# Row block 0 loaded and mapped in two halves of 256 rows, and column 0 of six row blocks begun on the first half

## What is computed

```python
x1  = layernorm(x + adj @ (x * (u >= 0.1) / 0.9))
m   = tanh(|x1|) * x1 / (|x1| + 1e-8)             # per row, |x1| clipped to 10
s   = adj @ m
out = arctanh(|s|) * s / (|s| + 1e-8)             # |s| clipped to 0.999
y   = layernorm(x1 + out @ weight + bias)
```

## Time and profile before

| | us |
|---|---|
| Median of 3 runs (lowest, highest) | 941.54 (941.12, 941.77) |
| The profiled execution, its own time | 944.53 |
| Its span in the profile | 941.9 |
| PE busy in the span | 898.6 (95%) |
| DVE busy | 287.2 (30%) |
| ACT, POOL busy | 52.2, 57.4 (6%, 6%) |
| Read from HBM | 355.57 MB, 380 GB/s over the span |

### The profile page before, as it was taken

The page is one execution under the profiler, slowest core; times in us unless marked ns, Lnnn a source line. Parts: engine busy times, 40 slices in busy tenths (PEclk is TensorE's granted clock), DMA queues, the critical chain, the costliest instruction groups (busy, mean ns, idle before and its releaser), DMA issues.

```text
span 941.9 us, 10555 instructions
## 1 busy us (share of the span) xinstructions
PE 898.6 (95%) x4224; PEld 301.8 (32%) x4224; DVE 287.2 (30%) x1056; ACT 52.2 (6%) x136; POOL 57.4 (6%) x50
## 2 busy tenths in 40 slices
PE   5579999999999999999999999999999999999994
PEld 1113333333333333333333333333333333333331
DVE  1136463422314130303131130403104030057565
ACT  0001010000000000000000000000000000002332
POOL 0000000000000000000000000000000000003232
PEclk9999999999999999999999999999999999999998
DMA  9999999999999999997979899898998999999993
GB/s 380 418 422 421 422 421 416 421 422 422 419 421 422 421 414 421 347 424 257 422 274 400 347 336 373 323 422 344 372 358 303 424 347 354 310 402 420 421 421 134
DMA packets 52319, 358.35 MB, mean 380 GB/s; under 512 B 6320, under 2 KB 8368, under 8 KB 9392
## 3 DMA queue, kind: packets, MB, share of 16 engines
q1 hardware_dynamic: 49536, 355.59, 93.5%
q10 hardware_dynamic: 2736, 2.10, 0.7%
HBM read 355.57 MB, written 2.10 MB: 380 GB/s over the span
## 4 chain that ended last, share of the span: by engine, by line
PE 85%; DMA 12%; SPq 2%; DVE 1%; issue 0%; POOL 0%; ACT 0%; DVEq 0%
PE sums_both L697 38%; PE sums_part L660 19%; PE sums_first L651 19%; DMA ring<-adj_dram 12%; PE sums_part L651 3%; PE sums_part L679 3%; PE sums_both L679 3%; SPq L339 1%; SPq L335 0%; PE sums_first L741 0%; PE sums_both L741 0%; PE sums_both L736 0%; POOL rooted L379 0%; POOL rooted L360 0%; DVE rows_in L603 0%
## 5 line engine op out<-in xcount | busy, mean ns | idle before, releaser
L697 PE MATMUL sums_both<-ring,feats 128*64 128x512 f32 x1696 | 370.2, 592 | 0.7 <-DMA ring<-adj_dram 0.7
L651 PE MATMUL sums_first<-ring,feats 128*64 128x512 f32 x1088 | 245.9, 598 | 27.7 <-DMA ring<-adj_dram 27.7
L697 PEld LDWEIGHTS sums_both<-ring,feats 128*64 128x64 f32 x1696 | 122.8, 137 | 242.3 <-issue 239.3
L660 PE MATMUL sums_part<-ring,feats 128*64 128x512 f32 x816 | 183.1, 593 | 1.0 <-issue 1.0
L651 PEld LDWEIGHTS sums_first<-ring,feats 128*64 128x64 f32 x1088 | 77.0, 138 | 190.0 <-issue 141.0
L487 DVE TENSOR_TENSOR row_saved<-sums_both,row_saved 64x512 f32<-64x512 f32 x15 | 10.2, 682 | 350.7 <-ACT row_saved L421 350.7
L660 PEld LDWEIGHTS sums_part<-ring,feats 128*64 128x64 f32 x816 | 59.3, 137 | 115.3 <-issue 114.7
L370 POOL TENSOR_TENSOR rooted<-base,power 128x8 f32<-128x8 f32 x16 | 27.8, 1736 | 801.1 <-DVE base L513 801.1
L552 DVE TENSOR_TENSOR rows_in<-sums_part,rows_in 128x512 f32<-128x512 f32 x36 | 24.9, 692 | 134.3 <-PE sums_part L660 134.2
L651 PE MATMUL sums_part<-ring,feats 128*64 128x512 f32 x240 | 55.9, 596 | 3.0 <-DMA ring<-adj_dram 3.0
L421 ACT COPY row_saved<-sums_first 64x512 f32<-64x512 f32 x16 | 9.3, 580 | 607.2 <-PE sums_first L651 607.2
(11 more groups left out here) (72 smaller groups left out, 246.6 us busy)
## 6 DMA issues: line engine op xcount, KB each, us to landing
ring<-adj_dram SPq DMA_DIRECT2D x331, 1024.0 KB, 12.9
rows_in<-xu_dram SPq DMA_DIRECT2D x8, 512.0 KB, 20.0
feats<-adj_dram SPq DMA_DIRECT2D x4, 1024.0 KB, 18.9
out_dram<-rows_in ACTq DMA_DIRECT2D x15, 128.0 KB, 7.5
out_dram<-rows_in SPq DMA_DIRECT2D x1, 96.0 KB, 1.9
selw<-selector_dram ACTq DMA_DIRECT2D x1, 32.0 KB, 6.7
selw<-weight_dram ACTq DMA_DIRECT2D x1, 32.0 KB, 10.3
bias_sb<-bias_dram ACTq DMA_DIRECT2D x1, 32.0 KB, 12.4
```

What stands on the lines that cost most here:

```text
L651: last = nc.tensor.matmul(bank[at:at + F], feats[:, which, c * TB + t, :], block_of(slot)[:, t, :], start=start and t < 2, stop=stop and t ...
L660: last = nc.tensor.matmul(bank[F * g:F * g + F], feats[:, 1, c * TB + t, :], block_of(slot)[:, t, :], start=start and t == 0, stop=stop an ...
L697: last = nc.tensor.matmul(sums_both[r % 2][layer * F:layer * F + F], feats[:, layer, c * TB + t, :], block_of(slot)[:, t, :], start=begin ...
```

## The change

Row block 0 is stored on the host in another layout: for each pair of columns and each half of 256 rows, a block of 1 MB. The first eight loads (`top`) hold rows 0 to 255 of all columns, the next eight rows 256 to 511, each with 8 matmuls of 256 columns; each half has a `turn` of its own with two tiles of 128 rows. After both, column 0 of rows 2 to 7 is begun on the first half of mapped rows (`begin`, 4 matmuls on the first half of the block, a load of 0.5 MB) in six different PSUM banks, and completed on the second (`complete`, the other 0.5 MB). The lead of row block 1 is dropped; `early` remains for rows 8 to 15. The held columns 0 to 3 of row 0 lie in pairs in two slots each, released after the odd column. Later re-reads of row 0 (`strip`) fetch two pieces of 4 KB for each partition. Early sums of the first product are no longer transposed and added to x: ACT copies them as they are into the part of `feats` that their rows will fill later, and DVE adds them at the join, before the row's last blocks are in.

```diff
+BEGUN = (2, 3, 4, 5, 6, 7)
+HALF = BS // 2
+HALF_TILES = TB // 2
@@ work_order
         if r == 0:
-            order += firsts + holds + [("turn", 0)]
+            for h in range(2):
+                order += [("top", 0, pair, h) for pair in range(NB // 2 - 1, -1, -1)] + [("turn", 0, h)]
+            order += [("begin", row, 0) for row in BEGUN] + [("complete", row, 0) for row in BEGUN]
             continue
-        lead, rest = lead_of([("both", r, c) for c in range(r >= 2, r - 1)] + firsts)
+        lead, rest = ([], firsts) if r == 1 else lead_of([("both", r, c) for c in range(r >= 2, r - 1)] + firsts)
...
-            early = [("early", row, 0) for row in range(2, NB)]
+            early = [("early", row, 0) for row in range(BEGUN[-1] + 1, NB)]
@@ place_blocks
+            if kind == "top":
+                h = step[3]
+                kept[r, c, h] = place("block", 0, 2 * c + h)
+                own = [kept[r, c, h]]
+                if c >= HELD[0] // 2:
+                    done += own
...
+            elif kind == "begin":
+                own = [place("lower", r, c)]
+                kept[r, c] = own[0]
+            elif kind == "complete":
+                own = [kept.pop((r, c))]
+                loads.append(("upper", r, c, own[0][0], 0))
+                done += own
@@ SP
-                sp.dma_start(block_of(slot), adj[r, c]).then_inc(block_loaded[slot], 16)
+                if kind == "block":
+                    sp.dma_start(block_of(slot), adj[r, c]).then_inc(block_loaded[slot], 16)
+                if kind == "strip":
+                    own = slice(c % 2 * HALF_TILES, (c % 2 + 1) * HALF_TILES)
+                    sp.dma_start(block_of(slot).rearrange("p (h t) w -> p h (t w)", h=2),
+                                 adj[0, c - c % 2:c - c % 2 + 2, :, own, :].rearrange("h p t w -> p h (t w)")
+                                 ).then_inc(block_loaded[slot], 16)
+                if kind == "lower":
+                    sp.dma_start(ring[:, slot, 0:HALF_TILES, :],
+                                 adj[r, c, :, 0:HALF_TILES, :]).then_inc(block_loaded[slot], 16)
+                if kind == "upper":
+                    sp.dma_start(ring[:, slot, HALF_TILES:TB, :],
+                                 adj[r, c, :, HALF_TILES:TB, :]).then_inc(rest_loaded[r], 16)
@@ ACT
-                if step[0] == "early":
+                if step[0] in ("complete", "early"):
 
                     act.wait_ge(block_released, uses[i][1])
-                    nc.scalar.copy(support[half(r), r // 2], early_banks[r % 2][F:P]).then_inc(early_saved, 1)
+                    nc.scalar.copy(early_sums(r)[0:F], early_bank(r)[0:F, 0:HALF])
+                    nc.scalar.copy(early_sums(r)[F:P], early_bank(r)[0:F, HALF:BS])
+                    nc.scalar.copy(support[half(r), r // 2], early_bank(r)[F:P]).then_inc(early_saved, 1)
@@ DVE
+            def early_join(i, r):
+
+                dve.wait_ge(early_saved, saved_at[r])
+                dve.wait_ge(block_released, uses[i][1])
+                for h in range(2):
+                    w = slice(h * HALF, (h + 1) * HALF)
+                    last = V.tensor_tensor(row_sum[:, w], sums_both[r % 2][0:F, w], early_sums(r)[F * h:F * h + F], ALU.add)
+                done(last)
...
-            def early_end(i, r):
-                dve.wait_ge(block_released, uses[i][1])
-                turn(early_banks[r % 2][0:F].rearrange("p (t n) -> p t n", n=P)).then_inc(early_turned, 1)
-                dve.wait_ge(early_turned, r - 1)
-                done(V.tensor_tensor(x_row(r), turned[:], x_row(r), ALU.add))
@@ PE
+                if kind == "top":
+                    h = step[3]
+                    pe.wait_ge(dropped, 1 + chunk_order.index(c))
+                    for col in (2 * c, 2 * c + 1):
+                        for t in range(TB):
+                            at = F * (t % 2)
+                            last = nc.tensor.matmul(sums_first[h][at:at + F, 0:HALF], feats[:, 0, col * TB + t, :],
+                                                    pack_of(slot)[:, col % 2, t, :],
+                                                    start=col == NB - 2 and t < 2, stop=col == 1 and t >= TB - 2)
...
+                if kind in ("begin", "complete", "early"):
...
+                    if kind == "complete":
+                        pe.wait_ge(rest_loaded[r], 16)
+                    pe.wait_ge(mapped, turn_of(0, kind != "begin"))
+                    for t in range(HALF_TILES if kind == "complete" else 0, HALF_TILES if kind == "begin" else TB):
```

More of the change, by code:

```diff
@@ L166, in place_blocks, with place @@
     times = [0] * (SLOTS + SPARES)
-    turned = spares = 0
+    placed = turned = spares = 0
+    def place(kind, r, c):
+        nonlocal placed
+        assert placed < SLOTS or placed - SLOTS < len(freed), "every slot is held"
+        slot = placed if placed < SLOTS else freed[placed - SLOTS]
+        times[slot] += 1
+        loads.append((kind, r, c, slot, max(0, placed - SLOTS + 1)))
+        placed += 1
+        return slot, times[slot]
     for i, step in enumerate(order):
@@ L173, in place_blocks @@
         rows, c = step[1:3]
-        held = []
+        held, done = [], []
         for r in rows if kind == "part" else (rows,):
-            if kind == "part" and step[6]:
-                slot, nth = kept.pop((r, c))
-            else:
[L179 to L190, removed]
+            if kind == "top":
[4 more added lines that the diff above has]
+                    done += own
+            elif kind == "part" and step[6] and r == 0:
+                own = [kept[0, c // 2, h] for h in range(2)]
+                if c % 2:
+                    done += own
+            elif kind == "part" and step[6]:
+                own = [kept.pop((r, c))]
+                done += own
+            elif kind == "begin":
+                own = [place("lower", r, c)]
+                kept[r, c] = own[0]
+            elif kind == "complete":
+                own = [kept.pop((r, c))]
+                loads.append(("upper", r, c, own[0][0], 0))
+                done += own
+            else:
+                own = [place("block" if r else "strip", r, c)]
+                if kind == "hold":
+                    kept[r, c] = own[0]
+                else:
+                    done += own
+            held.append(own)
+        freed += [slot for slot, _ in done]
+        count = len(done)
+        if turned == NB + 1 and kind == "part" and not spares:
             spares = SPARES
             freed += range(SLOTS, SLOTS + SPARES)
-        uses[i] = held, len(freed)
+            count += SPARES
+        uses[i] = held, len(freed), count
     return loads, uses
@@ L204, in build @@
     chunk_order = []
[L205 removed]
+    for _, _, c, _, _ in loads[:NB]:
         if c * TB // CHUNK not in chunk_order:
@@ L226, in saved_through, with turn_of @@
     def saved_through(r):
-        return min(1 + 2 * r, 2 + r)
+        return r + 3
+    def turn_of(r, h=1):
+        return r + h + 1
+    saved_at = {row: k + 1 for k, row in enumerate(s[1] for s in order if s[0] in ("complete", "early"))}
+    unsignalled = [i for i, (_, _, count) in uses.items() if order[i][0] == "part" and not count]
     with ExitStack() as es:
```

182 lines of the change are left out of this document (113 added, 69 removed).

## The result

| | before | after |
|---|---|---|
| Median of the runs (lowest, highest), us | 941.65 (941.12, 942.10), 4 runs | 946.49 (945.28, 948.49), 4 runs |
| Ratio after / before, 95% interval | | 1.0051 [1.0039, 1.0062] |
| The profiled execution, its own time | 944.53 | 945.28 |
| Its span | 941.9 | 943.4 |

The change makes the kernel slower by 0.51%, 4.8 us, outside the range that was given. So medians are compared with medians here, and profiles by the time of "both 4 1", the step at the gate.

The account below looks back on a forecast made before the run. A full DMA queue up to the landing of block (4, 1) at 206.63 us was taken to bound the kernel. Median 941.54 us, + 0 for the idle time, + 0.36 for smaller transfers, gave 941.9 us; range 940.0 to 944.5 us.

Parts of the forecast that it names:

- the gate: Landing of block (4, 1), load 77, at 206.63 us; PE can't be further at "both 4 1" than the bytes before it.
- What bounds it: Full DMA queue for the first 345 us, so block (4, 1) landing at 206.63 us sets PE's time; gain there 0.
- The idle time moves and is not removed: PE's 4 to 5 us saved after 53 us return as 5 to 5.5 us of waits before 207 us; net 0.
- Mapping, early sums, ACT, DVE, slots, 256-column matmuls at no cost: Row 0's mapping in halves, early sums, shared slots and shorter matmuls: each covered by lead or idle time, cost 0.
- Smaller transfers: Early halves before "both 4 1" and later re-reads of row 0: 0.18 us each, +0.36 us in sum.
- that block lands when it did: Block (4, 1), before "both 4 1": same bytes ahead in a never dry queue, so unchanged landing but for smaller transfers' cost.
- rival 3: Small pieces cost more, before "both 4 1" and in the tail: +3.0 us, 944.5 us; chance 0.09.
- The bound from above: Smaller transfers priced like output stores, 1.21 times as much per MB: 0.25 us a half, 6.0 us for 24.
- rival 4: The fixed cost of each of six added transfers stands open: 11.4 us more, 952.9 us; chance 0.02.
- Rival 1: PE's 4.95 us of idle time between 53.25 and 73.5 us is really removed: 936.6 us; chance 0.06.
- The unexplained pause: One block between 53.25 and 56.85 us took 1.11 us too long; it may fall away or come twice: 940.4 to 943.0 us.

Follow-up runs that it names:

- e6: Kernel before with blocks (1, 6) and (1, 7) left out of the loads but for 64 bytes a partition: 936.58 us, ratio 0.995.
- e11: Changed kernel with half blocks stored as closed runs and re-reads of row 0 in runs of 8 KB: 941.53 us, 1.0003 to before.
- e3: Changed kernel with the six early blocks loaded whole and re-reads of row 0 from a closed second copy: 941.68 us, 1.0004 to before.
- e4: Kernel before with column 0 of rows 2 to 7 fetched as two halves, one right behind the other: 941.66 us, ratio 1.0001.
- e10: Changed kernel with the early halves read in the same order from a copy with 12 KB between partition rows: 943.29 us, 1.0018 to before.
- e5: Changed kernel with each early half block stored as a closed run of 512 KB, order kept: 943.33 us, 1.0014 to before.
- e1: Changed kernel with each of the six early blocks loaded whole, in one transfer of 1 MB: 943.24 us, 1.0011 to before.
- e7: Changed kernel with each second half of an early block loaded right behind its first half: 942.72 us, 1.0014 to before.
- e2: Changed kernel with row 0 re-read from a second copy in runs of 8 KB, early halves unchanged: 944.48 us, 1.0033 to before.
- e12: e11 with column 1 of rows 11 to 15 moved from behind the gate to before it: 937.75 us, 0.9964 to before.

## Why the prediction was wrong

**What bounds it: right.** The queue to block (4, 1) sets the time (e6: -4.84 us at the gate, -4.8 us at the end), and whatever is lost behind it comes on top.

**The idle time moves and is not removed: right.** PE runs without a break from 56.02 to 76.6 us; in the profile of after it waits 7.4 us for DMA before 345 us instead. Some eight short waits between 140 and 207 us were expected: after has 11 with 5.6 us there, since the late gate adds its share, and e11, where the gate is in place, has 9 with 4.4 us.

**Mapping, early sums, ACT, DVE, slots, 256-column matmuls at no cost: right.** No wait of PE for ACT or DVE; the second half's last mapped rows were written at 63.78 us, where 64.8 was allowed. The timeline of PE in after, at the last `top` step and the first `begin`:

```profile
54.24 1.95 PE L788 MATMUL sums_first<-ring,feats 128*64 128x256 f32 x16 [0.54 <-DMA ring<-adj_dram]
56.02 3.60 PE L804 MATMUL sums_both<-ring,feats 128*64 128x512 f32 x16
```

Eight matmuls of 256 columns took 1.78 us to the next start, where four of 512 take 1.72: 0.06 us of the 1.1 us allowed. e3 shows that all these together are free, to within the 0.1% of its interval.

**Smaller transfers: the step that failed.** The term was +0.36 us, 0.015 for each of 24 halves, "because the nearest row has the very size of piece". The whole change measures +4.8 us, and e3 and e11, which differ from after in these transfers alone, are within 0.2 us of before: all of it stands in this term. The size was right and was not what counted: e4 has the same halves at no cost. I had taken "size of the transfer" for the property of which the price depends, and the x and u pieces for the nearest row, though they stand singly between whole blocks and have a pitch of 32 KB. The halves of the change read every other 4 KB, and come six first ones in a row and then six second ones. In 54 to 74 us that cost 8.41 - 7.75 = 0.66 MB against before, 1.6 us at 421 GB/s, and 17.63 - 15.32 = 2.3 us against e10 and e5. With it fell the sentence "that block lands when it did": it landed 3.8 us later in the profile, of which e1, e5, e7 and e10 take back 3.2 to 4.0. About 3.2 us of the median are the halves; the rest, 1.6 us, is put down to the re-reads, six of which were priced at 0.18 us. As a mechanism this is nearest to rival 3, whose +3.0 us stood at 0.09, but not as it was put: the cost is no fixed price of each piece, it falls on a few of the twelve halves and, smaller, on the re-reads behind the gate. The bound from above in the prediction, 6.0 us, held; the choice of 0.36 within it failed.

**The fixed cost of added transfers (rival 4, 952.9 us): wrong.** e4 adds six transfers to before and e7 adds six to e1: +0.2 us (ratio 1.0001), and -0.5 us. The figure of about 2 us behind this rival, from the Trainium skill, "DMA: Bandwidth & Descriptors", section "Anatomy of one DMA", is given there for DMAs issued from GpSimd; these are issued from SP. **Rival 1 (936.6 us): wrong,** as e11 shows, which removes the idle time and ends at 941.53.

**The unexplained pause** between 53.25 and 56.85 us coincides with a fetch of instructions. The DMA queues of before, 54 to 56 us:

```profile
q1 hardware_dynamic: 114, 0.81, 98.5%
q8 instruction: 1, 0.02, 3.4%
```

The fetch is one packet of 16 KB that took 3.4% of 16 x 2 us = 1.1 us, which is the 1.11 us by which the block was late. That a block waits for its slowest engine would explain it, but no run isolates it, and most fetches go without such a pause: before has five more of 16 KB until 187 us, and beside them one block is 0.3 us late and no other by more than 0.2; e5, e7 and e10 have one at 53.2 to 53.4 us and lose at most 0.2 us there.

**Where the 3.8 us at the gate lie,** by landing times: after's 16 blocks of row 0 were in 1.0 us later than before's (54.20 against 53.21 us), the next 7 MB took 1.6 us more, although they lack before's pause of 1.1 us, and the 54 blocks from there to the gate 1.2 us more. In that last part two landings of after are 3.15 and 3.31 us behind the one before, at 159.87 and 193.03 us; e2 has the same two (3.16 and 3.35), while e5, e7 and e10 have none over 2.7 us there. Fetches of instructions started at 157.9 and 189.1 us in after, but the other kernels have fetches near there too. So e5, e7 and e10 take back these 1.4 us as well, and why is not shown.

**Open.** The mechanism in the memory; why stalls among the halves are followed by two more pauses 90 and 120 us later; and how much of the re-reads' 1 to 2 us is real. after's four runs spread over 3.2 us, no more than the 27 runs of before that were taken beside e1, which spread over 3.7.

One slip in the sums: the range for the pause, 940.4 to 943.0 us, has its lower end from 941.54 us and its upper from 941.9; from 941.9 the lower is 940.8. Nothing hangs on it.

## What to carry to other kernels

Where PE waits for a full queue, idle time that is removed ahead of the waiting step comes back before that step; look for steps with more compute per byte to move there (e12, -3.6 us against before), and only then is the gap worth closing. Price a new transfer by its address pattern as well as by its size: what is left out between the pieces, at which pitch, and how many such transfers stand in a row. If only part of a block is needed first, store the parts as closed runs, or pad the pitch.

## What was not expected of the hardware

- Twelve transfers that read 4 KB at a pitch of 8 KB, six first halves and then six second halves, took 17.63 us and ran at 387 GB/s (54 to 74 us), where at a pitch of 12 KB the same bytes in the same order took 15.32 us and ran at 414. With each second half right behind its first, the pitch of 8 KB cost nothing (413).
- Halves of 0.5 MB in closed runs, paired, or at 12 KB pitch run at 413 to 414 GB/s behind one another, against 420 for whole blocks: a little less, and not visible in the median of e4.
- One instruction fetch is a packet of 16 KB that takes 1.1 us, 0.07 us per KB; a sixteenth of a block (64 KB in 2.49 us) takes 0.04.
